# Finished rows are normalised, stored, turned and gated inside the layers' block, and the routing one-hots are kept in pairs

## The reference

```
x = _layernorm(x)                      # 3125 nodes x 256 features
h = acc = x                            # graph part, 50000 weighted edges
for _ in range(3):
    h = segment_sum(edge_weight * h[src], dst)     # a sparse matrix times h
    h = h / max(norm(h), 1e-12)
    acc = acc + h
x1 = x_in + acc / 4
y = _layernorm(x1)                     # "y" below: the tokens
logits = y @ gate_w + gate_b           # 16 experts
top2 values -> softmax weights; top2 indices -> experts
moe = sum of the two experts' relu(y @ w1 + b1) @ w2 + b2, weighted
out = x1 + _layernorm(y + moe) * gamma + beta
```

## Time and profile before

| | us |
|---|---|
| median of 3 runs | 1477.4 |
| the profiled execution's own time | 1478.73 |
| its span, first to last instruction | 1477.0 |
| outside its span | 1.7 |
| TensorE busy over the span | 1305.6 (88%) |
| DVE busy | 1076.6 (73%) |
| ACT busy | 888.7 (60%) |

### The profile page before, as it was taken

How to read it: one execution, slowest core, us unless ns; L and a number is a source line. 1 busy time by engine, 2 the same in 40 slices (tenths; PEclk the granted TensorE clock), 3 DMA queues, 4 the chain that set the end, 5 groups by cost and what they waited for, 6 DMA issues and landing times. The chain is left out here.

```text
span 1477.0 us, 31300 instructions
## 1 busy us (share of the span) xinstructions
PE 1305.6 (88%) x9556; PEld 1160.0 (79%) x9562; DVE 1076.6 (73%) x1899; ACT 888.7 (60%) x1985; POOL 235.4 (16%) x207
## 2 busy tenths in 40 slices
PE   4577777777799999999999999999969799999985
PEld 1477777777778888888888888888855699999964
DVE  8988889888777555766565765566657598888857
ACT  1788888888855554655544655545542366666653
POOL 1300000000021000000000000000000588888620
PEclk9798999999999999999999999999987699999998
DMA  5288888888886666656666656666611598989662
GB/s 190 64 210 193 194 196 200 204 198 205 215 256 207 186 178 195 186 163 186 186 176 197 183 165 185 179 195 183 182 54 37 193 310 262 287 269 279 220 202 96
DMA packets 236494, 283.03 MB, mean 192 GB/s; under 512 B 16270, under 2 KB 173046, under 8 KB 236422
## 3 DMA queue, kind: packets, MB, share of 16 engines
q1 hardware_dynamic: 228741, 261.28, 63.1%
q0 software_dynamic: 7680, 20.98, 5.1%
HBM read 194.27 MB, written 87.93 MB: 191 GB/s over the span
## 5 line engine op out<-in xcount | busy, mean ns | idle before, releaser
L869 PE MATMUL ps_rows<-h_both,a_high 128*128 (+1 forms) x1875 | 507.0, 399 | 12.3 <-ACT halves L604 5.3
L696 DVE TENSOR_TENSOR a_low<-a_raw,a_high 128x640 fp32r<-128x640 f32 x375 | 305.7, 824 | 233.4 <-ACT a_high L590 230.1
L590 ACT ACTIVATE a_high<-a_raw 128x640 fp32r<-128x640 f32 x375 | 274.4, 740 | 290.0 <-PE ps_rows L872 268.6
L869 PEld LDWEIGHTS ps_rows<-h_both,a_high 128*128 128x128 f32 x1875 | 331.1, 191 | 70.4 <-ACT halves L604 14.4
L872 PEld LDWEIGHTS ps_rows<-h_both,a_low 128*128 128x128 f32 x1875 | 276.3, 191 | 32.6
L872 PE MATMUL ps_rows<-h_both,a_low 128*128 (+1 forms) x1875 | 284.8, 283 | 0.0
L834 PE MATMUL ps_w<-lo_hot,key_w 128*120 128x160 bf16 x2736 | 236.9, 247 | 36.8 <-DVE key_w L680 36.8
L834 PEld LDWEIGHTS ps_w<-lo_hot,key_w 128*120 128x120 bf16 x2736 | 223.9, 141 | 42.8 <-ACT key_w L563 35.4
L1406 POOL DMA_INDIRECT x_t<-tokens,r_token x80 | 104.1, 1301 | 731.3 <-POOLq L891 707.5
L572 ACT ACTIVATE win<-ps_w 128x480 f32<-128x480 f32 x304 | 147.9, 570 | 53.7 <-PE ps_w L839 35.7
L680 DVE TENSOR_TENSOR key_w<-key_hot,tab_marks 128x1440 bf16<-128x1440 bf16 (+1 forms) x228 | 164.5, 776 | 0.0
(11 more groups left out here) (244 smaller groups left out, 1544.4 us busy)
## 6 DMA issues: line engine op xcount, KB each, us to landing
a_raw<-a_rows SPq DMA_DIRECT2D x375, 320.0 KB, 3.2
a_rows<-win SPq DMA_DIRECT2D x228, 240.0 KB, 3.6
w_raw<-in_L_ffn_w SPq DMA_DIRECT2D x80, 512.0 KB, 7.2
a_rows<-win SPq DMA_DIRECT2D x76, 180.0 KB
b_t<-in_L_ffn_b SPq DMA_DIRECT2D x40, 128.0 KB, 4.9
found<-results SPq DMA_DIRECT2D x6, 640.0 KB, 9.5
hf<-in_x SPq DMA_DIRECT2D x1, 3072.0 KB
x<-in_x SPq DMA_DIRECT2D x1, 3072.0 KB
```

The lines of the kernel that those rows point to most:

```text
L590: a.activation(a_high[:, u, :], a_raw[:, u, :], ACT.Copy).then_inc(high_split, 1)
L696: v.tensor_tensor(a_low[:, u, :], a_raw[:, u, :], a_high[:, u, :].bitcast(F32), ALU.subtract).then_inc(low_split, 1)
L869: nc.tensor.matmul(ps[:, banks[w][r], :], a_high[:, u, r * P:(r + 1) * P], both, start=first, stop=False, skip_group_check=True)
```

## The change

In the last layer, three groups of slots are added after each pass `w`. At `t` = 12 DVE aggregates the moments of the pass's five chunks. At 13 ACT takes the root. At 15 DVE works out the shift and normalises the odd chunks; at 17 ACT normalises the even ones. SP stores the five chunks' `y` between loads of A, one pass later. The gate's weights and bias are loaded before the last layer.

After the last step, TensorE turns and gates in pairs of chunks: ten pairs (chunks 0 to 19) that are complete by then, in PSUM banks that the last pass does not use, and then three pairs (20 to 24). DVE copies out pairs 0 to 4, woven into its joins of the last pass and ahead of its clamp; ACT copies the others, pairs 5 to 9 ahead of the last pass's root. The search runs in sets of 20 and 5 chunks. Tiles that were in `phase_route` now lie in the old window buffer (`win` in the names). `phase_route` begins with `gap`; TensorE there first waits for the bias load and then has 16 matmuls on zeros where it had 11 and 42.

The one-hots' layout becomes `[P, 25, 128, 2]`: a choice's column is read with a step of two elements. The pieces are of 6, 6, 6 and 7 pairs; they were of 12, 13, 12 and 13 choices.

```
@@ phase_layers, SP
             for j in range(RING, SPR):
-                load(s.LAYERS - 1, j)
+                load(LAST_LAYER, j)
+                if j >= 2 * CH and j % CH == 3:
+                    store_y(j // CH - 2)
+            for w in (PASSES - 2, PASSES - 1):
+                store_y(w)
+            sp.dma_start(tail, y[0:s.REST, s.FULL, :]).then_inc(y_stored, 16)
+            sp.wait_ge(y_stored, 16 * (PASSES + 1))
@@ phase_layers, ACT, slot
+                if last and w >= 0 and t == RING + 8:
+                    if w == PASSES - 1:
+                        for n in range(BY_DVE, EARLY):
+                            copy_turned(n)
+                    deviations(w)
+                if last and w >= 0 and t == RING + 12:
+                    normalise(w)
...
+            for n in range(EARLY, PAIRS_Y):
+                copy_turned(n)
@@ phase_layers, DVE, join
                 for r, c in enumerate(chunks(w)):
+                    if isinstance(layer, int) and layer == LAST_LAYER and w == PASSES - 1 and r in TURNS_AT:
+                        copy_turned(TURNS_AT.index(r))
@@ phase_layers, DVE
+            def shifts(w):
+                r = slice(w * G, (w + 1) * G)
+                dve.wait_ge(mv_ready, w + 1)
+                dve.wait_ge(std_ready, w + 1)
+                rsqrt(v, link_chain, rstd[:, r], std[:, r], mv[:, r, 1], fix_y[:, r])
...
+            def copy_turned(n):
+                dve.wait_ge(turned, n + 1)
+                if n >= consts.YT:
+                    dve.wait_ge(gated, n - consts.YT + 1)
+                v.tensor_copy(yT[:, n % consts.YT, 0:wide(n)], ps[:, turn_bank(n), 0:wide(n)]).then_inc(yt_by_dve, 1)
@@ phase_layers, DVE, slot
                 if w >= 0 and t == RING + 3:
+                    if last and w == PASSES - 1:
+                        for n in range(len(TURNS_AT), BY_DVE):
+                            copy_turned(n)
                     clamp(layer, w)
...
+                if last and w >= 0 and t == RING + 7:
+                    aggregate(w)
+                if last and w >= 0 and t == RING + 10:
+                    shifts(w)
+                    normalise(w)
@@ phase_layers, PE, after the steps
+            pe.wait_ge(const_ready, 3)
+            pe.wait_ge(gates_in, 32)
+            pe.wait_ge(evacuated, (s.LAYERS + 1) * CH - G)
+            for n in range(2):
+                turn(n)
+            for n in range(EARLY):
+                gate(n)
+                if n + 2 < EARLY:
+                    turn(n + 2)
+            pe.wait_ge(evacuated, (s.LAYERS + 1) * CH)
+            for n in range(EARLY, PAIRS_Y):
+                turn(n)
+            for n in range(EARLY, PAIRS_Y):
+                gate(n)
@@ phase_route
-        lo_hot = sb("lo_hot_s", [P, P, K2], BF16)
-        hi_hot = sb("hi_hot_s", [P, NS, K2], BF16)
-        hi_no = sb("hi_no_s", [P, 2, NS, K2], BF16)
+        lo_hot = sb("lo_hot_s", [P, CH, P, 2], BF16)
+        hi_hot = sb("hi_hot_s", [P, CH, NS, 2], BF16)
+        hi_no = sb("hi_no_s", [P, CH, 2, NS, 2], BF16)
...
+            pe.wait_ge(consts_in, 16)
+            idle(16)
             pe.wait_ge(counts, 1)
...
-                    ins = t.matmul(ps_s[:, 0:2 * NS], lo_hot[:, :, j], hi_no[:, :, :, j].rearrange("p a b -> p (a b)"),
+                    ins = t.matmul(ps_s[:, 0:2 * NS], lo_hot[:, j // 2, :, j % 2],
+                                   hi_no[:, j // 2, :, :, j % 2].rearrange("p a b -> p (a b)"),
                                    start=(j == 0), stop=(j == K2 - 1))
```

More of the change, by code:

```diff
@@ L617, in roots, with deviations, normalise @@
                 a.activation(root[:, r], ssq[:, r], ACT.Sqrt).then_inc(rooted, 1)
+            def copy_turned(n):
+                act.wait_ge(turned, n + 1)
+                if n >= consts.YT:
+                    act.wait_ge(gated, n - consts.YT + 1)
+                a.activation(yT[:, n % consts.YT, 0:wide(n)], ps[:, turn_bank(n), 0:wide(n)],
+                             ACT.Copy).then_inc(yt_by_act, 1)
+            def deviations(w):
+                r = slice(w * G, (w + 1) * G)
+                act.wait_ge(mv_ready, w + 1)
+                a.activation(std[:, r], mv[:, r, 1], ACT.Sqrt).then_inc(std_ready, 1)
+            def normalise(w):
+                act.wait_ge(shift_ready, w + 1)
+                for c in chunks(w):
+                    if c % 2 == 0:
+                        act.wait_ge(summed, s.LAYERS * CH + c + 1)
+                        a.activation(y[:, c, :], x1[:, c, :], ACT.Identity, bias=shift[:, c:c + 1],
+                                     scale=rstd[:, c:c + 1]).then_inc(y_even, 1)
             def slot(layer, j, last):
@@ L802, in _ @@
                 slot(s.LAYERS - 1, j, True)
+            for k in range(len(SETS)):
+                best_two(k)
         @block.tensor
@@ L885, in _, with turn, gate, phase_route @@
                         step(layer, w, CH - RING + u, u, False, u == RING - 1)
-def phase_route(nc, s, consts, moments, x1, y, gate_w, gate_b, b1, routes, y_dram):
+            def turn(n):
+                for c in range(2 * n, min(2 * n + 2, CH)):
+                    pe.wait_ge((y_odd if c % 2 else y_even), c // 2 + 1)
+                    for k in range(KD):
+                        at = ((c % 2) * KD + k) * P
+                        ins = nc.tensor.transpose(ps[:, turn_bank(n), at:at + P], y[:, c, k * P:(k + 1) * P],
+                                                  consts.ident[:, :])
+                ins.then_inc(turned, 1)
+            def gate(n):
+                wait_copied(pe, n)
+                for c in range(2 * n, min(2 * n + 2, CH)):
+                    k_set = 0 if c < FIRST else 1
+                    at = (c - SETS[k_set].start) * E
+                    for k in range(KD):
+                        src = ((c % 2) * KD + k) * P
+                        ins = mm(ps[:, SET_BANK[k_set], at:at + E], yT[:, n % consts.YT, src:src + P], gw[:, k, :],
+                                 start=(k == 0), stop=(k == KD - 1))
+                ins.then_inc(gated, 1)
+            pe.wait_ge(const_ready, 3)
[12 more added lines that the diff above has]
+                gate(n)
+def phase_route(nc, s, consts, b1, routes):
     with ExitStack() as ctx:
@@ L1002, in _ @@
             a = nc.scalar
[L1003 to L1010, removed]
[L1011 to L1018 removed]
             act.wait_ge(gap_ready, 1)
             a.activation(ex[:], gap[:], ACT.Exp).then_inc(exp_ready, 1)
[L1021 removed]
+            for n, pairs in enumerate(PIECES):
                 act.wait_ge(hi_hot_ready, n + 1)
[L1023 to L1024 removed]
+                a.activation(hi_no[:, pairs, 1, :, :], hi_hot[:, pairs, :, :], ACT.Copy,
+                             scale=e_part[:]).then_inc(numbered, 1)
             act.wait_ge(b1_ready, 1)
```

258 lines of the change are left out of this document (119 added, 139 removed).

## The result

The changed kernel takes 1453.5 us (median of 4 runs, 1449.86 to 1457.61), the kernel before 1475.6 (4 runs, 1466.23 to 1478.03). The ratio is 0.987, with a 95% interval of 0.984 to 0.990. In five later rounds (experiment 9) it was 0.985 (0.981 to 0.989). The forecast was 1461, with a range of 1452 to 1468. The profiled execution took 1449.86 us, the lowest of the four; its span is 1448.0.

The account below looks back on a forecast made before the run. It took the 74 us chain of hand-overs between last step and experts, with three waits ending on TensorE, as the bound; 9.4 + 0 + 0.8 + 6.4 = 16.6 us off 1477.4 gave 1461 us, range 1452 to 1468.

Parts of the forecast that it names:

- Three waits that ended last on TensorE: Between last step and experts: turning and gating, the zeros before the counts, and the 50 one-hot matmuls bound the stretch.
- Part 1: Last layer: the added work costs 0, covered by slack; without slack at most 13 us.
- The slack of 5.4 us per tile: Last layer: time a tile has to spare before it is wanted, said to cover the added work.
- Rival 3: Last layer: the added work starves TensorE and the kernel gets slower, 1485 us; chance 4%.
- Part 2: Tail from the last step to `gap`: 9.4 us gained, with ends of 7.4 and 15.8.
- Clock falling about 5 us in: Tail: the case chosen, clock dropping to half at 1088.7, `gap` at 1112.1, 9.4 us earlier.
- the full-clock end: Tail: the case of full clock throughout, `gap` at 1105.7, 15.8 us earlier.
- Part 3: Zeros before the counts: counts taken 7.6 us behind `gap`, 0.8 us gained.
- Part 4: One-hots in pairs: matmuls at 0.14 us each instead of 0.30, 6.4 us gained.
- Rival 1: Tail, counts and one-hots: full clock through the tail, 24.8 us gained, 1452.6 us; chance 15%.
- Rival 2: One-hots: the pairs don't pay, only 10.3 us gained in all, 1467 us; chance 13%.
- rival 4: Whole kernel: a hold-up or late root cancels the gains, 1476 to 1478 us; chance 4%.

Follow-up runs that it names:

- experiment 9: The changed kernel unaltered, and with two reorderings, five rounds each on one chip: 1478.6 and 1468.8 us against 1497.0, ratios 0.985 and 0.981.
- the two repeats: The kernel before and the changed kernel, each run once more unaltered: 1469.68 us for the one profiled, and ratio 0.985 for the other.
- change_again: The changed kernel run once more, unaltered: 1478.6 us against 1497.0 for the kernel before, ratio 0.985.
- pairs_only: The kernel before with only the one-hots' new layout in pairs: 1497.3 us against 1505.6, ratio 0.9952.
- far_weights: The changed kernel with only the weights of the 50 matmuls back at a step of 50 elements: slots start 10.63 us behind the first one-hot.
- woven_zeros: The changed kernel with one 512-column matmul on zeros behind each gate from pair 2 on: 1458.1 us against 1464.1 for the kernel before.
- late_turn: The changed kernel with TensorE's first turn waiting for all evacuations of the last pass: 1496.0 us, ratio to the kernel before 0.9935.
- late_filled: late_turn with 13 matmuls on zeros filling the wait: one profiled execution, `gap` 31.17 us behind the last step.

## Why the forecast came out where it did

*What bounds it.* Three waits that ended last on TensorE were named; all three gave time, and nothing outside them did.

*Part 1, the last layer: right.* From its first step to its last, the last layer took 222.83 us before (860.57 to 1083.40) and 223.03 after (853.87 to 1076.90); the two repeats took 222.79 and 223.01. The price is 0.2 us. The slack of 5.4 us per tile covered DVE's added pieces. Rival 3 is out.

*Part 2, the tail: the mechanism right, the size off; this is the mis-sized term.* 9.4 us was taken and 15.3 measured in the profile. The step that failed is "Clock falling about 5 us in". The sub-steps for that case were good, as change_again shows, where the clock fell at 6.0: turn 9's end at 16.9 us behind the last step (worked out: 17.6), ACT's root at 17.4 (18.1), `gap` at 28.3 (28.7), a gain of 9.9. But in four of the five executions of this tail the clock fell at 12.6 or later, and there the gain is 15.3 to 15.9, next to the 15.8 of the full-clock end. I had taken the wait of the first gates for DVE's copies as a reason for an early fall; it was 0.35 us of idle (11.65 us busy of 12.00) and did not bring one. A single row of the before profile (a fall 13.7 us into the same instructions) was also taken for the rule, where pairs_only kept the clock up to the last gate. What was left out of the sum is that the fall is not a fixed property of the program but differs from one execution to the next; it should have stood as a spread, which the five executions put at 10 to 16 us. The smaller pieces held: clamp 5.97 us behind the last step (6.6 worked out), copies 0.69 on DVE (0.7) and 0.60 on ACT (0.5).

*Part 3, the counts: the size right, in part by luck.* 0.7 us against 0.8. The two terms under it were both off and all but cancelled: the bias had landed and the zeros began 1.8 us behind `gap`, where 2.3 was taken, and with the clock back only 5.0 us into them, where 3.6 was taken, the zeros took 6.0 us and not 5.2. The term moves with the clock: in change_again the counts were taken 6.84 us behind `gap`, in far_weights 7.81.

*Part 4, the pairs: right.* 6.6 against 6.4. The last piece's 14 matmuls took 1.19 us at full clock, and 2.08 at half in far_weights, the 2.0 worked out. The reason given, the step of 50 elements, holds for the moving operand alone; it was not told apart in the prediction. The Trainium skill's page "SBUF — State Buffer", section "Specifications (TRN2)", wants at least two hits in each 16-byte line for full bandwidth: a step of 50 bf16 elements has one, a step of two has four. The moving operand agrees (0.29 against 0.15 us); the weight load shows no such price, and there the measurement decides.

*Rivals.* Rival 1 was given 15% with the condition "full clock throughout". That condition was not met in after (0.50 from 1089.5), but its gain in the tail came nearly whole, 15.3 us of 15.8, though not the one in the counts, 0.7 of 2.6. TensorE's last five gates at half clock cost 1.9 us (4.29 against 2.40 in woven_zeros) and were partly beside DVE's search. The rule of the Trainium skill, "TensorE: Matmul & The Clock Gate", section "Part 1: The HAM clock gate", that the clock follows how busy TensorE has been, agrees with the trace on one side: behind late_turn's 2.84 us of idling the clock fell. On the other it does not, since 19.56 busy us of 20 in change_again stayed at 0.50. Rival 2 is out by pairs_only (6.6 us), rival 4 by that and by part 1, where nothing was held up.

*The sum.* 15.3 + 0.7 + 6.6 = 22.5 (rounded terms), against 22.1 between the medians. The forecast was 7.5 us high: 5.9 of it from part 2, and most of the rest from the kernel before, whose median went from 1477.4 to 1475.6 with a fourth run. The measured 1453.5 lies outside the forecast's own 1457 to 1463. It lies in the stated 1452 to 1468 because that range was drawn to reach rival 1, whose 1452.6 it all but meets.

## What to carry to other kernels

Light work on TensorE set right behind dense work, with no gap between, kept the full clock here for 6.0 to 15.8 us; with a wait of 2.84 us for one semaphore more in between, all but its first half microsecond ran at half, and the tail was 12.8 us longer. Where a term hangs on where the clock falls, profile the same kernel several times before taking one fall for the rule, and carry the whole spread into the sum. For a product of one-hots, look at the step of the moving operand first; at this size and at half clock the weights' step cost nothing.

## What was not expected of the hardware

- The clock's fall behind the same instructions came 6.0, 12.6, 15.7, 15.7 and 15.8 us behind the last dense step in five executions. In the turning and gating of before it came after 13.7 us in two executions and in pairs_only after 17.3, behind the last gate. In late_filled and woven_zeros it came 6.0 and 5.9 us behind the last matmul of 512 columns, as far as behind the last step in change_again. What decides it was not found.
- Once the clock was at half, turning and gating did not bring it back: 19.56 us busy of 20.00 at 0.50 in change_again, 29.22 of 31.10 in late_turn. With one matmul of 512 columns behind each gate from pair 2 on it stayed for 20.8 us, in the one execution made.
- With 160 columns and a step of 50 bf16 elements, the moving operand doubles a matmul at half clock (0.29 against 0.15 us); 128 columns of weights at that step cost nothing that shows (14 matmuls in 2.08 us against 2.05).
- With the last gates at full clock (woven_zeros) the tail did not get shorter: DVE's search of the first 20 chunks had become its bound.
